# Keeping values in SBUF between projection and attention, loading the first heads ahead, and placing two small vector steps in later halves

## The reference

```
h   = attention_tok(x)                     # 512 x 512 softmax per head, all keys
h   = [cls_tok ; h]                        # 513 tokens
h  += attention_rot(layernorm(h))          # rotary positions, causal softmax
h  += moe(layernorm(h))                    # 8 experts, top 2
a   = top32_attention(layernorm(h))        # causal scores, only the 32 largest of a row kept, softmax, times v
h  += a @ Wo.T + bo
gate = selu(layernorm(h) @ wi + bi) @ wo + bo   # 256 logits; the two largest of a row are searched
out = h, with the last experts for rows whose index falls below 8
```

## Time and profile before

| what | value |
|---|---|
| time, median of 3 runs | 2076.37 us (2073.16 to 2081.22) |
| the profiled execution | 2070.6 us |
| its span in the trace | 2068.9 us |
| PE, DVE, ACT, POOL busy | 71%, 69%, 41%, 28% of the span |
| "tok" projection and attention | about 17 to 330 us |
| "rot" projection and attention | about 370 to 697 us |
| first experts | about 760 to 1063 us |
| gather and projection of image 0 | 1065 to 1128 us |
| top attention | 1128 to 2062 us |

### The profile page before, as it was taken

How to read it: one execution, slowest core, us unless ns; L and a number is a source line. 1 busy time by engine, 2 the same in 40 slices (tenths; PEclk the granted TensorE clock), 3 DMA queues, 4 the chain that set the end, 5 groups by cost and what they waited for, 6 DMA issues and landing times. The chain is left out here.

```text
span 2068.9 us, 35074 instructions
## 1 busy us (share of the span) xinstructions
PE 1463.6 (71%) x10419; PEld 861.5 (42%) x10420; DVE 1434.8 (69%) x4683; ACT 840.3 (41%) x2077; POOL 579.0 (28%) x1039
## 2 busy tenths in 40 slices
PE   6498988967888650999952477766666677766664
PEld 3122224434444440566631244544444444544543
DVE  3587885656777550111138799989989999899871
ACT  2165665214555410222212444444444545454432
POOL 4100000320000006000024344544555545555440
PEclk9699999987999965999976557767776767676676
DMA  4672230253322412111134100200013001300000
GB/s 158 179 259 81 73 89 9 73 163 90 75 77 53 189 64 83 40 46 46 46 123 129 58 27 27 67 18 9 19 27 82 2 26 35 94 12 1 1 1 12
DMA packets 87487, 137.64 MB, mean 67 GB/s; under 512 B 9720, under 2 KB 68000, under 8 KB 85540
## 3 DMA queue, kind: packets, MB, share of 16 engines
q1 hardware_dynamic: 84068, 127.38, 20.9%
q0 software_dynamic: 3264, 8.41, 1.3%
HBM read 82.50 MB, written 53.76 MB: 66 GB/s over the span
## 5 line engine op out<-in xcount | busy, mean ns | idle before, releaser
L1586 DVE MATCH_REPLACE8 top_left<-top_next,top_left 128x65 f32<-128x65 f32 (+15 forms) x768 | 322.6, 428 | 0.0
L1581 DVE MAX8 top_next<-top_left 128x8 f32<-128x65 f32 (+15 forms) x768 | 301.1, 433 | 0.0
L1494 POOL TENSOR_TENSOR top_e<-top_e,top_left 128x129 f32<-128x129 f32 (+15 forms) x256 | 191.0, 767 | 207.4 <-DVE top_left L1586 207.4
L1311 ACT ACTIVATE top_e<-top_ps_s,top_neg_max 128x129 f32<-128x129 f32 (+15 forms) x256 | 125.0, 488 | 245.7 <-POOL top_neg_max L1479 238.8
L667 DVE TENSOR_REDUCE tok_rowmax<-tok_ps_s 128x1 f32<-128x512 f32 x256 | 166.9, 688 | 42.6 <-PE tok_ps_s L509 40.0
L2152 DVE TENSOR_TENSOR moe_hid<-moe_act_gate,moe_ps_h 128x512 f32<-128x512 f32 x39 | 26.8, 688 | 220.1 <-ACT moe_act_gate L2113 220.1
L1154 PE MATMUL top_ps_pt<-ident,top_e 128*128 128x128 f32 x640 | 144.1, 356 | 36.3 <-issue 33.5
L667 DVE TENSOR_REDUCE rot_rowmax<-rot_ps_s 128x1 f32<-128x128 f32 (+3 forms) x256 | 115.7, 487 | 46.6 <-PE rot_ps_s L512 42.7
L640 ACT ACTIVATE tok_et<-tok_ps_st 128x1024 f32<-128x1024 f32 x128 | 124.2, 1021 | 51.2 <-PE tok_ps_st L543 51.2
L2052 PE MATMUL moe_ps_h<-moe_w,moe_rows_t 128*128 x312 | 142.5, 600 | 0.2 <-issue 0.2
L1154 PEld LDWEIGHTS top_ps_pt<-ident,top_e 128*128 128x128 f32 x640 | 104.8, 185 | 66.4 <-issue 60.0
(11 more groups left out here) (342 smaller groups left out, 3134.7 us busy)
## 6 DMA issues: line engine op xcount, KB each, us to landing
moe_w<-in_moe_w SPq DMA_DIRECT2D x3, 4096.0 KB, 24.5
moe_xs<-zeros SPq DMA_DIRECT2D x1, 5120.0 KB, 20.6
last_xs<-zeros SPq DMA_DIRECT2D x1, 5120.0 KB, 33.5
moe_rows<-moe_xs SPq DMA_DIRECT2D x40, 128.0 KB
moe_ys<-moe_y SPq DMA_DIRECT2D x38, 128.0 KB, 1.7
v_rows<-tok_va SPq DMA_DIRECT2D x4, 1024.0 KB, 5.1
tok_vs<-v_rows SPq DMA_DIRECT2D x16, 256.0 KB
v_rows<-rot_va SPq DMA_DIRECT2D x4, 1024.0 KB, 5.0
```

The source lines that it names most:

```text
L1311: act.activation(e[:, U % KEPT, 0:keys(U)], row(U), ACT.Exp, bias=neg_max[:, U % 4:U % 4 + 1]).then_inc(e_ok, 1)
L1494: pool.tensor_tensor(e[:, U % KEPT, 0:w], e[:, U % KEPT, 0:w], left[:, U % 4, 0:w], ALU.subtract).then_inc(prob_ok, 1)
L1581: dve.max(next8[:, U % 2, step // 2, :], left[:, U % 4, 0:keys(U)]).then_inc(pick, 1)
L1586: ins = dve.match_replace(left[:, U % 4, 0:w], next8[:, U % 2, step // 2 - 1, :], left[:, U % 4, 0:w], 0.0)
```

## The change

Three edits go together.

1. **Values stay in SBUF.** A new class `Heads` owns `parts`, `va`, `qs`, `ks`, `vs` and their semaphores across `project` and `attend`. The store to `v_rows` and the 16 loads from it are gone in both attentions; POOL copies each step's v from `va` to `vs`, one instruction a step, behind the same `pv_mm` wait. `project` no longer waits for its stores at its end; `attend`'s SP waits for them per step.
2. **First loads ahead.** SP issues the q and k loads of steps 0 and 1 of "tok" and "rot" inside `project`, between the stores of images 2 and 3; `gather_project` issues those of step 0 of the top attention. POOL sets the ones of all four `ks`; PE waits for them only before `turn_neg`; the class-token matmuls and the first scores no longer wait. The 20 mask copies of DVE move to the start of `gather_project`'s DVE list.
3. **Later halves.** In the planner `moments` is not placed in a half that begins less than 2.0 (planner units) after the residual is done, and `search` is put in the first free half that begins at least 3.0 after `add_bias`, while the ROUTED pipeline goes on with the next tile.

```diff
@@ project, sync queue
-                sp.wait_ge(v_ok, 2 + (b + 1) * NQ)
-                sp.dma_start(c.vd[b], va[:, b, :, :, :, :].rearrange("p g n h s -> p g (n h s)")
-                             ).then_inc(v_out, 16)
-            sp.wait_ge(v_out, 16 * B)
-            for i in range(4):
-                sp.wait_ge(stored[i], 16 + B * step_stores)
+                    if (b, k) in ((2, 0), (2, 3)):
+                        g = k // 3
+                        sp.wait_ge(stored[0], 16 + step_stores)
+                        load_queries(sp, c, 0, g, heads.qs[g], heads.loaded[g])
+                    elif (b, k) in ((2, 1), (3, 0)):
+                        g = b - 2
+                        sp.wait_ge(stored[2], 16 + step_stores)
+                        load_keys(sp, c, 0, g, heads.ks[g], heads.loaded[g])
@@ attend, sync queue
-                load_step(sp, c, b, g, qs[g], ks[g], loaded[g])
-                sp.dma_start(vs[g][:, :, :].rearrange("p n w -> p (n w)"), c.vd[b, :, g, :]).then_inc(v_loaded[g], 16)
+                if s >= heads.ahead:
+                    sp.wait_ge(heads.stored[g // 2], 16 + STEP_STORES * (b + 1))
+                    load_queries(sp, c, b, g, qs[g], loaded[g])
+                    sp.wait_ge(heads.stored[2 + g // 2], 16 + STEP_STORES * (b + 1))
+                    load_keys(sp, c, b, g, ks[g], loaded[g])
@@ attend, gpsimd
-            for i in range(2, G):
+            for i in range(G):
                 pool.memset(ks[i][PARTS * HD:P, :, :], 1.0).then_inc(ready, 1)
+            pool.wait_ge(ready, G)
+            for s in range(B * G):
+                b, g = s // G, s % G
+                if s >= G:
+                    pool.wait_ge(pv_mm, 2 + NQ * (s - G + 1))
+                pool.tensor_copy(vs[g][:, :, :], va[:, b, g, :, :, :].rearrange("p n h s -> p n (h s)")
+                                 ).then_inc(v_loaded[g], 1)
@@ attend, tensor and vector
-            pe.wait_ge(ready, G + 1)          # was ahead of the first matmul
+            pe.wait_ge(ready, G)              # now ahead of turn_neg(0, 0)
-            for i in range(2):
-                dve.memset(ks[i][PARTS * HD:P, :, :], 1.0).then_inc(ready, 1)
-            dve.wait_ge(ready, G + 1)
@@ attend_top, planner
+                    if name == "moments" and free + 2.0 > begins[half] and half < 2 * rounds:
+                        break
+                    if name == "search" and half < 2 * rounds:
+                        later = half + 1
+                        while begins[later] < free + 3.0 or (name, later) in step_of:
+                            later += 1
+                        step_of[name, later] = T
+                        run[:] = T + 1, 0, max(free, begins[half])
+                        continue
@@ attend_top, sync queue
-                        load_step(sp, c, b, g, qs[g], ks[g], loaded[g])
+                        if b or g >= heads.ahead:
+                            load_step(sp, c, b, g, qs[g], ks[g], loaded[g])
@@ gather_project, sync queue
+            sp.wait_ge(stored, 16 * 2 * QUARTERS)
+            for g in range(heads.ahead):
+                load_step(sp, c, 0, g, heads.qs[g], heads.ks[g], heads.loaded[g])
             sp.wait_ge(v_out, 16 * (G + 1))
-            sp.wait_ge(stored, 16 * 2 * QUARTERS)
```

More of the change, by code:

```diff
@@ L70 @@
 EARLY = 3
+STEP_STORES = 16 * 2
 FINISH_AFTER = 4
@@ L169, in _, with __init__, load_parts, load_queries @@
                 pool.wait_ge(filled, 19)
-def load_step(sp, c, b, g, q, k, loaded):
[L175 to L186, removed]
+class Heads:
+    def __init__(self, c, stack, tag, width, ahead):
+        self.ahead = ahead
+        if ahead > 1:
+            self.parts = c.sbuf(stack, f"{tag}_parts", [P, SPLIT, 4, S + 1], BF16)
+            self.va = c.sbuf(stack, f"{tag}_va", [P, B, G, NQ, HG, STRIP], F32)
+            self.stored = [c.sem(c.stack, f"{tag}_stored{i}") for i in range(4)]
+        self.qs = [c.sbuf(stack, f"{tag}_qs{i}", [P, HG, S], BF16) for i in range(G)]
+        self.ks = [c.sbuf(stack, f"{tag}_ks{i}", [P, HG, width], BF16) for i in range(G)]
+        self.vs = [c.sbuf(stack, f"{tag}_vs{i}", [P, NQ + (1 if ahead == 1 else 0), P], F32) for i in range(G)]
+        self.loaded = [c.sem(c.stack, f"{tag}_loaded{i}") for i in range(G)]
+        self.v_loaded = [c.sem(c.stack, f"{tag}_v_loaded{i}") for i in range(G)]
+def load_parts(sp, dst, parts, runs, loaded):
+    at = 0
+    for part, n, times in runs:
+        rows = slice(at * HD, (at + n * times) * HD)
+        src = parts[part:part + n].rearrange("i d h t -> (i d) h t")
+        if times > 1:
+            src = parts[part:part + 1].broadcast_to([times, HD, HG, dst.shape[2]])
+        sp.dma_start(dst[rows, :, :], src).then_inc(loaded, 16)
+        at += n * times
+def load_queries(sp, c, b, g, q, loaded):
+    load_parts(sp, q, c.qd[b, g], Q_RUNS, loaded)
+def load_keys(sp, c, b, g, k, loaded):
+    load_parts(sp, k, c.kd[k.shape[2]][b, g], K_RUNS, loaded)
+def load_step(sp, c, b, g, q, k, loaded):
+    load_queries(sp, c, b, g, q, loaded)
+    load_keys(sp, c, b, g, k, loaded)
+def project(c, tag, w, qkb, vb, cls, heads, rope=None):
     nc = c.nc
@@ L220, in project @@
         lo_ok = c.sem(st, f"{tag}_lo_ok")
-        stored = [c.sem(st, f"{tag}_stored{i}") for i in range(4)]
+        stored = heads.stored
         v_mm = c.sem(st, f"{tag}_v_mm")
@@ L410, in attend @@
     with c.stage() as st:
-        qs = [c.sbuf(st, f"{tag}_qs{i}", [P, HG, S], BF16) for i in range(G)]
-        ks = [c.sbuf(st, f"{tag}_ks{i}", [P, HG, S + k0], BF16) for i in range(G)]
-        vs = [c.sbuf(st, f"{tag}_vs{i}", [P, NQ, P], F32) for i in range(G)]
+        qs, ks, vs, va = heads.qs, heads.ks, heads.vs, heads.va
         et = c.sbuf(st, f"{tag}_et", [P, 2, HG, S], F32)
@@ L433, in attend @@
         ctx_t = ps_pv[:, :].rearrange("p (n h s) -> p n h s", h=HG, s=STRIP)
-        loaded = [c.sem(st, f"{tag}_loaded{i}") for i in range(G)]
-        v_loaded = [c.sem(st, f"{tag}_v_loaded{i}") for i in range(G)]
+        loaded, v_loaded = heads.loaded, heads.v_loaded
         ready = c.sem(st, f"{tag}_ready")
+        neg_clear = c.sem(st, f"{tag}_neg_clear")
         vcls_mm = c.sem(st, f"{tag}_vcls_mm")
@@ L802, in attend_top @@
     with c.stage() as st:
-        qs = [c.sbuf(st, f"{tag}_qs{i}", [P, HG, S], BF16) for i in range(G)]
-        ks = [c.sbuf(st, f"{tag}_ks{i}", [P, HG, WIDE], BF16) for i in range(G)]
-        vs = [c.sbuf(st, f"{tag}_vs{i}", [P, NQ + 1, P], F32) for i in range(G)]
+        qs, ks, vs = heads.qs, heads.ks, heads.vs
         raw8 = c.sbuf(st, f"{tag}_raw8", [P, 4, 8], F32)
@@ L855, in attend_top @@
         ps_x = c.psum(st, f"{tag}_ps_x", [P, S])
-        loaded = [c.sem(st, f"{tag}_loaded{i}") for i in range(G)]
-        v_loaded = [c.sem(st, f"{tag}_v_loaded{i}") for i in range(G)]
-        masks_ok = c.sem(st, f"{tag}_masks_ok")
+        loaded, v_loaded = heads.loaded, heads.v_loaded
         s_mm = c.sem(st, f"{tag}_s_mm")
@@ L1006, in attend_top @@
             half += 1
-        LAST_ROUND = half // 2 + 1
+        LAST_ROUND = max(h for _, h in step_of) // 2 + 1
         def bank_free(eng, name, T):
@@ L2661, in _, with gather_project @@
                 pool.memset(c.h[:, NT, :], 0.0).then_inc(cleared, 1)
-def gather_project(c, tag, came, w, qkb, vb, weight, fetch, ahead):
+def gather_project(c, tag, came, w, qkb, vb, weight, fetch, ahead, heads):
     nc = c.nc
@@ L3006, in program @@
             load_patches(c, a["x_t"], a["cls"], get_tok)
-            project(c, "tok", *w_tok, cls=False)
-            attend(c, "tok", causal=False, clear=True, fetch=get_rot)
+            with ExitStack() as near:
+                heads = Heads(c, near, "tok", S, 2)
+                project(c, "tok", *w_tok, cls=False, heads=heads)
+                attend(c, "tok", causal=False, heads=heads, clear=True, fetch=get_rot)
             attend_out(c, "tok", a["tok_wo"], a["tok_bo"], residual=False, cls=False)
-            project(c, "rot", *w_rot, cls=True, rope=tables)
-            attend(c, "rot", causal=True)
+            with ExitStack() as near:
+                heads = Heads(c, near, "rot", S + 1, 2)
+                project(c, "rot", *w_rot, cls=True, heads=heads, rope=tables)
+                attend(c, "rot", causal=True, heads=heads)
             w13 = c.sbuf(wide, "moe_w13", [P, DC, E, 2 * MOE_HIDDEN], F32)
```

42 lines of the change are left out of this document (21 added, 21 removed).

## The result

The changed kernel takes **2019.4 us**, the median of 4 runs (2013.2 to 2024.9); the kernel before, in the same comparison, 2075.1 us, the median of 4 (2073.2 to 2081.2). The ratio is 0.9726, 95% interval 0.9691 to 0.9761. Forecast were 2027 us and 2003 to 2056. The profiled execution took 2019.0 us with a span of 2017.3 (before 2068.9), 51.6 us less; the terms forecast for it come to 47.1.

What follows compares the result with a forecast made beforehand. No engine bounds the whole kernel; DVE bounds the top attention, PE the first experts, and borders stand idle. Terms -19.3 - 14 + 8 - 7.5 + 2 - 28.5 + 12.2 = -47.1 us; forecast 2027 us, range 2003 to 2056.

Steps and rivals of the forecast that it cites:

- Border tok: First projection to first attention: no end wait for v's store, first loads early; -18.3 us, -19.3 with v traffic.
- SP's 12 more issues inside the projection: First projection: 6.2 us of added load issues before stores awaited one image later; cost nothing, bounds 0 to 2 us.
- 68.4 us for the first scores: Start of tok's attention: first scores forecast at about 68.4 us, in place of 86.70.
- The zero fills: Tok: less v traffic ahead of 10 MB of zero fills may shorten one PE wait by 0 to 2.5 us; -1.
- Border rot: Second projection to attention: earlier start and no wait for keys, class-token scores at 454.5 not 468.58; -14 us.
- The copies of v: Rot: POOL's copies hold up two-input DVE instructions, 12 steps at 0.7 us, +8, bounds 0 and 18; tok nothing.
- Gather: Before the top attention: DVE's 20 mask copies delay POOL's first gathers, between nothing and 6.4 us; +2 taken.
- Border top: Start of top attention: group 0's keys loaded ahead, later groups one place earlier; -7.5 us, bounds -5 and -12.
- Planner, main part: Top attention: nearly all 33.9 us of moments and search waits go, a fifth returns as score waits; together -28.5 us.
- the stalls change their name: Rival, top attention: score waits grow by what POOL waits lose; main part gains 5 not 28.5, 2050 us; chance 0.2.
- The other rivals: Both attentions collide 2050 (0.1); no collision 2019 (0.1); planner ineffective 2055 (0.05); slower TensorE clock in first experts (0.04).
- Planner, tail: End of top attention: deferred moments push tile 15's chain back, turn_context of tile 16 at 2045.6 not 2033.40; +12.2 us.

Runs made afterwards that it cites:

- the best kernel: Changed kernel with only step 0's q and k loads ahead, behind the last image's first two stores, in tok and rot: 2016.4 us, ratio 0.9729.
- the five kernels named above: Changed kernel rerun (2019.5 us); planner rules undone (2045.1); search rule alone (2038.0); each v copy doubled (2023.0); early loads behind last image's stores (2017.8).
- margin 1.0: Changed kernel with the planner's margin for moments at 1.0 us in place of 2.0: 2017.4 us, ratio 0.9730.
- the three kernels with a shorter tail: On changed kernel: moments rule only below half 180, 2021.4 us; moments margin 1.0, 2017.4; margin 0.5 with later copies and step 0 alone ahead, 2005.3.
- the copies' edit alone: Changed kernel with POOL's v copies from step 4 on waiting for one more group of values: 2005.3 us, ratio 0.9666.

## Why the prediction was right, and where it was not

*Border tok: the step that failed.* I had put "SP's 12 more issues inside the projection" at nothing with "0 to 2 us as bounds". They cost about 7. Six of their loads, those of step 0, stand in the one queue ahead of image 2's stores of keys, and ACT awaits the first of these for image 3: issued at 55.21, it was not all there before 66.1. Of the 32 arrivals that its semaphore counts 26 were in by 59.1, and the last six came between 62.5 and 66.1; before the change the same store's 32 lay within 1.3 us. I looked at the issues' time and not at the packets behind them, though DVE and ACT kept waiting for stores in that queue. The Trainium skill ("DMA: Bandwidth & Descriptors", section "Queues, rings and completion order") says that each DMA engine takes the descriptors of a ring in their order; the trace agrees: ACT's wait is 8.33 us, and no wait of ACT there is over 1.5 us once the loads stand behind. The experiments showed more than the trace: three limits lie within 2 us of each other here, ACT's wait, SP's issues and the keys' landing, and to remove one uncovers the next. My 68.4 us for the first scores would need 19.4 us behind image 2's first store; the best kernel had 23.1.

*The zero fills.* Forecast -1, measured -1.9 for the whole of B; in later runs of the same code B was 229.1 to 233.0, so nothing can be read from it.

*Border rot.* -14 forecast, -14.1 measured, and -13.3 to -15.1 in all but the kernel with loads behind the last store.

*The copies of v.* +8 forecast and +8.8 measured, by two errors that cancel, so by luck. The copy takes 0.62 us and not 1.09, so a step pays 0.33 us on the average of 12 in its instructions and not 0.7. What I left out was that a later negation makes DVE wait for scores, 0.37 us more. The mechanism is shown by the copies moved away, in D and in the instructions, and by the copies doubled, in the instructions alone. The Trainium skill ("SBUF — State Buffer", section "Who interferes with whom") has it that whoever issues first keeps the shared ports for its whole instruction. The trace agrees: L726, 0.18 us alone, ends 0.03 us behind the copy, and with two copies the next ends 0.03 behind the second. In tok the prediction of nothing holds.

*Gather.* +2 forecast; 0.8 measured in the profiled execution, 2.0 to 2.4 in others. The experts end 17.0 us earlier (DVE's last copy there at 1043.87, before 1060.90), and from that copy to the first gathered rows it is 15.7 us (1059.58), before 14.9 (1075.84). The first three gathers took 1.36, 1.26 and 1.25 us to issue in place of 1.05, 1.01 and 0.99, and 4.6 us of mask copies lay beside them: here they slip in between. But in the five kernels named above, in which the first gather takes 4.24 us, it ends 0.13 us behind the last mask copy, and those 14.9 us are 16.9 to 17.3. The Trainium skill's rule ("SBUF — State Buffer", section "SBUF: two separate sides"), that GpSimd can't write descriptors during such a copy, agrees with these five, in which it stands until the whole row of copies is over, and in direction with the others. What decides between the two is open. The +2 was a choice between bounds, and it fell right for the slower case.

*Border top.* As forecast: the second group of keys came 11.0 us behind the first (forecast 12), DVE's first two waits for them were 0.5 and 6.2 us (near 0 and 5), and E fell by 6.8 against -5.5 for the two terms; other runs of the same code give 463.6 to 469.9 for E.

*Planner, main part.* -28.5 forecast, -36.7 measured. Wrong was "I let a fifth come back": none did, and scores cost less. The likely reason is the 34 matmuls that went into the tail: with margin 1.0 they stay in F, scores cost 30.6 us, about as before (29.5), and F is 825.0, 29.1 below the kernel before and close to the forecast. My rival, that the stalls change their name, is refuted by its own measure: scores 24.9 us, not 40. The other rivals fell with the rows above.

*Planner, tail.* +12.2 forecast, +10.2 measured, at the place forecast: `route` of 14 behind the last take, `turn_context` 9.7 us later against it. But I booked it as a pure loss. Each of the three kernels with a shorter tail (59.7, 58.8, 55.9) has an F that is 7.6 us or more longer than the changed kernel's, and the time stays (2021.4 and 2017.4 against 2019.5; 2005.3 against 2005.3 with the copies' edit alone): it was for the most part work that the main part no longer has to bear.

So the total was right within 8 us partly by luck: the 7 us missing at one border were made up by 8 in the main part, and the two have nothing to do with each other.

## What to carry to other kernels

A load put ahead into a running stage isn't free because its issue is short: ask which store stands behind it in the queue and who awaits that store, then what the issuing engine itself still has to put out before the stage can end. A copy on GpSimd is to be timed by what VectorE does at that moment: one event later, among reductions out of PSUM, the same copies cost nothing and not 10 us. And a longer tail behind a saturated stretch is no loss by itself; cut both spans at the same event before trying to get it back.

## What was not expected of the hardware

Steps of the same code take one of two lengths: in rot 13.3 to 14.3 us or 14.7 to 15.8, in changing places, so that D was 211.0 to 218.2 us in kernels in which nothing there differs. With the copies moved away they are 13.3 to 14.2 nearly throughout, and D is 204.2, 204.3 and 205.4. The collision itself is the same in both: in the changed kernel L726 takes 0.46 us in a step of 15.0 us and in the next one of 13.8, but DVE stands still for 4.0 us in the first and 2.9 in the second, most of it before maxima. I did not find what decides it. The first gather beside the mask copies has two lengths as well, 1.36 and 4.24 us.
